# Four-layer image kernel: a head without early fillers, the first result added from its PSUM bank, and the places of all steps drawn anew

## The reference

```
x = x + moe(norm(x))        # layer 0: 2x2 patches (128 values), router over 8 experts, the best 2 of them,
                            #          (v * sigmoid(g)) @ w2[e], where v, g are the halves of patch @ w1[e]
x = x + deform(norm(x))     # layer 1: 3x3 convolution gives offsets and masks; 9 taps x 4 corners are
                            #          gathered at the offsets, weighted, multiplied by w; batch norm, relu
x = x + s4d(norm(x))        # layer 2: encoder to 256, state-space convolution (16 taps), gelu, gated linear
                            #          unit, layer norm, decoder
x = x + mixer(norm(x))      # layer 3: depthwise 7x7, channel norm, 32 -> 128 gelu -> 32, layer scale
```

## Time and profile before

| | us |
|---|---|
| runs (median, lowest, highest) | 1696.59, 1690.04, 1696.91 |
| profiled execution: its own time | 1698.67 |
| profiled execution: span from first to last instruction | 1696.9 |
| first gather starts | 58.26 |
| last gather starts | 1585.30 |
| PE, DVE, ACT, POOL busy | 1339.8, 1006.1, 541.9, 1180.7 |
| 1,152 gathers, busy and mean | 1155.8, 1.003 |

### The profile page before, as it was taken

How to read it: one execution, slowest core, us unless ns; L and a number is a source line. 1 busy time by engine, 2 the same in 40 slices (tenths; PEclk the granted TensorE clock), 3 DMA queues, 4 the chain that set the end, 5 groups by cost and what they waited for, 6 DMA issues and landing times.

```text
span 1696.9 us, 13775 instructions
## 1 busy us (share of the span) xinstructions
PE 1339.8 (79%) x4164; PEld 611.3 (36%) x4164; DVE 1006.1 (59%) x1809; ACT 541.9 (32%) x870; POOL 1180.7 (70%) x1187
## 2 busy tenths in 40 slices
PE   8778566999849958879969848789849644898797
PEld 7543233444324413324334313334224211343345
DVE  4546765544662479943655588845433794445785
ACT  2122212323332331243423412342413304244345
POOL 1477777756777777777777778777777777777700
PEclk9889877999969979989979979989869876899899
DMA  7233223421322222322332223322221112222000
GB/s 254 64 82 84 79 66 84 118 61 56 92 78 73 65 57 77 90 75 56 86 97 59 62 62 84 92 64 70 61 76 53 50 53 59 81 64 68 22 10 16
DMA packets 109609, 123.06 MB, mean 73 GB/s; under 512 B 49952, under 2 KB 85856, under 8 KB 109408
## 3 DMA queue, kind: packets, MB, share of 16 engines
q0 software_dynamic: 36864, 75.57, 15.8%
q1 hardware_dynamic: 71712, 43.40, 10.0%
q10 hardware_dynamic: 960, 3.21, 0.5%
HBM read 101.89 MB, written 9.01 MB: 65 GB/s over the span
## 4 chain that ended last, share of the span: by engine, by line
PE 37%; POOL 25%; DVE 20%; issue 10%; ACT 5%; DMA 2%; SPq 1%; DVEq 0%; POOLq 0%; ACTq 0%
POOL gt L1042 25%; PE bank L1991 7%; PE bank L2004 6%; DVE rb L1742 5%; PE bank L1941 4%; PE bank L1905 4%; PE bank L1901 3%; PE bank L1915 3%; DVE gt L1626 3%; PE bank L1974 2%; DVE he L1524 1%; PE bank L2027 1%; DVE gt L1628 1%; PE bank L2048 1%; PE bank L1805 1%
## 5 line engine op out<-in xcount | busy, mean ns | idle before, releaser
L1042 POOL DMA_INDIRECT gt<-corner_table,idx x1152 | 1155.8, 1003 | 422.3 <-issue 347.3
L1991 PE MATMUL bank<-u,wk 128*128 128x512 f32 x512 | 240.4, 614 | 3.7 <-DMA u<-sqb 3.7
L2004 PE MATMUL bank<-yg,wts 128*128 128x512 f32 x512 | 234.3, 602 | 0.4 <-DVE rb L1682 0.2
L1626 DVE TENSOR_TENSOR gt<-gt,bank 128x1152 f32<-128x1152 f32 x128 | 172.6, 1349 | 88.2 <-DMA gt<-corner_table,idx 87.1
L1905 PE MATMUL bank<-xg,w_sb 128*128 128x512 f32 (+1 forms) x256 | 135.3, 612 | 45.1 <-DVE xg L1515 23.3
L1961 PE MATMUL bank<-cst,sm 128*128 128x128 f32 x384 | 75.9, 313 | 118.1 <-DVE sm L1634 117.9
L1668 DVE SCALAR_TENSOR_TENSOR tg<-tg,ae 128x512 f32<-128x512 f32 x64 | 44.1, 692 | 198.2 <-ACT ae L1218 198.2
L1742 DVE SCALAR_TENSOR_TENSOR rb<-xp,par,rb 128x1024 f32<-128x1024 f32 x124 | 155.0, 1291 | 0.0
L1991 PEld LDWEIGHTS bank<-u,wk 128*128 128x128 f32 x512 | 97.3, 197 | 121.7 <-issue 114.7
L1524 DVE SCALAR_TENSOR_TENSOR he<-he,bank 128x512 f32<-128x512 f32 (+1 forms) x128 | 83.0, 651 | 92.0 <-PE bank L1905 88.8
L2004 PEld LDWEIGHTS bank<-yg,wts 128*128 128x128 f32 x512 | 95.2, 192 | 111.5 <-issue 109.4
(11 more groups left out here) (283 smaller groups left out, 1512.5 us busy)
## 6 DMA issues: line engine op xcount, KB each, us to landing
gt<-corner_table,idx POOLq DMA_INDIRECT x1152
tb<-gate_of_token SPq DMA_DIRECT2D x56, 256.0 KB, 4.9
u<-sqb SPq DMA_DIRECT2D x48, 128.0 KB, 2.8
corner_table<-tb SPq DMA_DIRECT2D x36, 128.0 KB, 2.7
w_sb<-w ACTq DMA_DIRECT2D x6, 512.0 KB, 7.1
xp<-x_patch SPq DMA_DIRECT2D x4, 512.0 KB, 4.4
X<-x SPq DMA_DIRECT2D x1, 1536.0 KB, 9.2
out<-X SPq DMA_DIRECT2D x6, 256.0 KB, 2.2
```

What stands on the lines that cost most here:

```text
L1042: pool.indirect_dma_start(gt[:, t % GRING, k].rearrange("p a c -> p (a c)"), None, corners, bass.IndirectOffsetOnAxis(ap=idx[s % 2][:, j, ...
L1626: ch.then(tt(rows, rows, share.unsqueeze(2).to_broadcast([P, 4 * KK, C]), ALU.mult))
L1991: op = mm(psum[b][:, :], wk[:, t, d], u4[:, g, at:at + HALF], start=t == 0, stop=t == JJ - 1 and n > 0)
L2004: op = mm(psum[B2.bank(*name)][:, :], w_glu[:, k, col + d * P:col + (d + 1) * P], yg[:, c % 2, k], start=k == 0, stop=k == NB2 - 1)
```

## The change

It has three parts; the last words of its description, on the depthwise taps, say that these stay as they were, and no line of the diff touches them.

- **Head.** `l0_norm` loses its first `keep(3, 20)`, and the one behind it goes from 10 to 5; `pass0_out` loses `keep(3, 10)`; the one ahead of the first `l1_conv` goes from 28 to 14. On VectorE the multiplications by the shares become `pass0_gated`, the first of them ahead of the last `pass0_he`. SP loads `X[:, 0]` behind the weights instead of ahead of them and `X[:, 1:]` only behind `l0_shares(1)`; the wait for it moves from `load_conv` to pass 3's `l0_tail`. Six of the 18 table clears are issued before SP waits for the gates.
- **First result.** `l0_collect(0)` goes, on ScalarE and SP: in `l0_tail` VectorE adds the four 32x256 quarters of bank 2 straight to X.
- **Places.** Most numbers of `PL` are new; pass 3's places no longer have the lower bound `h2`.

```diff
-PL = {'k1': 8.5, 'k2': 13.5, 'cut': 20, 'u1': 1.4, 't1': 2.0, 'h1': 5.5, 'u2': 5.9, 'c2': 9.5, 't2': 11.4, 'h2': 14.8, 'r3': 15.3, 'u3': 15.8, 'c3': 18.5, 'ub': 5.2, 'uc': 13.8, 'tail': 23.9, 'headend': 27.8, 'route': 26.8, 'route2': 33.1, 'bstart': 1.2, 'bend': 10.7, 'cend': 21.0, 'ahead': 16.2, 'astart': 22.4, 'aend': 31.7, 'a0head': 18.7, 'zbstart': 3.4, 'zbend': 6.4, 'zcend': 15.5, 'zahead': 16.7, 'zastart': 19.2, 'zaend': 26.5, 'zchead': 24.5, 'zcstart': 25.8, 'zcstop': 31.6, 'last2': 9, 'a0start': 19.7, 'a0end': 34, 'c30': 23.1, 'tail0': 25.1, 'headend0': 29, 'bhead': 0.5, 'head': 24.8, 'b1': 3.8, 'e3': 7, 'd3': 0.7, 'c0': 2.1, 'c1': 5.8, 'e4': 9.5, 'd4': 0.6, 'f0': 9.3, 'f1': 9.6, 'f2': 12.2, 'f3': 13, 'd5': 0.8}
+PL = {'k1': 1.57, 'k2': 9.76, 'cut': 26, 'u1': 0, 't1': 1.94, 'h1': 5.87, 'u2': 6.02, 'c2': 7.22, 't2': 9.7, 'h2': 12.8, 'r3': 10.56, 'u3': 13.02, 'c3': 19.53, 'ub': 6.18, 'uc': 13.8, 'tail': 24.74, 'headend': 28.99, 'route': 26.95, 'route2': 33.1, 'bstart': 1.11, 'bend': 10.7, 'cend': 21.96, 'ahead': 16.2, 'astart': 23.16, 'aend': 31.7, 'a0head': 20.3, 'zbstart': 0.44, 'zbend': 6.4, 'zcend': 20.18, 'zahead': 16.85, 'zastart': 21.52, 'zaend': 26.33, 'zchead': 24.85, 'zcstart': 26.43, 'zcstop': 30.35, 'last2': 9, 'a0start': 22.35, 'a0end': 32.5, 'c30': 22.05, 'tail0': 24.06, 'headend0': 28.27, 'bhead': 0.5, 'head': 26.66, 'b1': 3.8, 'e3': 7, 'd3': 0.7, 'c0': 2.1, 'c1': 5.8, 'e4': 9.5, 'd4': 0.6, 'f0': 9.3, 'f1': 9.6, 'f2': 12.2, 'f3': 13, 'd5': 0.8}
...
-    for u in range(2, PAIR):
+    for u in range(2, PAIR - 1):
         parts += value[u:u + 1] + first[u + 5:u + 6]
+    parts += [("pass0_gated", 0)] + value[PAIR - 1:] + [("pass0_gated", e) for e in range(1, NE)]
...
-        put(heads(1), (g("c2") + .2, g("c2") + .3, 1), (max(g("r3"), g("h2") + .2), max(g("u3"), g("h2") + .7), 2))
-        put(units_a(3), (max(g("u3"), g("h2") + .7), g("c30")))
+        put(heads(1), (g("c2") + .2, g("c2") + .3, 1), (g("r3"), g("r3") + .7, 2))
+        put(units_a(3), (g("u3"), g("c30")))
...
-        parts = first_pass() + [("load_conv",), ("l0_collect", 0), ("l0_tail", 0)] + head_a(0)
+        parts = first_pass() + [("load_conv",), ("l0_tail", 0)] + head_a(0)
...
-    some += [(g("c0"), *fourth[0])] + spread(taps, [(g("c1"), g("c2"), len(taps))])
+    some += [(g("c0"), *fourth[0])] + spread(taps, [(g("c1"), 9.5, len(taps))])
...
-            sp.dma_start(X[:, 0], x_v[:, 0]).then_inc(S["x0_in"], 16)
...
+                sp.dma_start(X[:, 0], x_v[:, 0]).then_inc(S["x0_in"], 16)
                 sp.dma_start(wts[:, :], weights).then_inc(S["wts_in"], 16)
                 sp.dma_start(bb[:, :, :].rearrange("p t m -> p (t m)"), places).then_inc(S["wts_in"], 16)
                 sp.dma_start(wenc[0:NB2 * C, :], w_enc[0:NB2 * C]).then_inc(S["wts_in"], 16)
-                sp.dma_start(X[:, 1:NS], x_v[:, 1:NS]).then_inc(S["x_in"], 16)
+
+            def clear_tables(t):
+
+                sp.dma_start(tables[1, t], tb[:, 0, 0]).then_inc(S["table_zero"], 16)
+                sp.dma_start(tables[0, t][:, 1:GI], tb[:, 0, 0, 1:GI]).then_inc(S["table_zero"], 16)
 
...
+                if a == 0:
+                    sp.wait_ge(S["zeros_set"], 1)
+                    for t in range(TQ // 3):
+                        clear_tables(t)
                 sp.wait_ge(S["gate_out"], 16 * (a - SPLIT + 2 if a else 1))
                 if a == 0:
                     for i in range(NE):
                         spread_share(sp, a, i)
-                    sp.wait_ge(S["zeros_set"], 1)
-                    for t in range(TQ):
-                        sp.dma_start(tables[1, t], tb[:, 0, 0]).then_inc(S["table_zero"], 16)
-                        sp.dma_start(tables[0, t][:, 1:GI], tb[:, 0, 0, 1:GI]).then_inc(S["table_zero"], 16)
+                    for t in range(TQ // 3, TQ):
+                        clear_tables(t)
...
+                if a == 1:
+                    sp.dma_start(X[:, 1:NS], x_v[:, 1:NS]).then_inc(S["x_in"], 16)
 
...
-                collect_patches(sp, a, PASSES[a][1], range(PT) if a else (0,))
+                collect_patches(sp, a, PASSES[a][1], range(PT))
 
...
-                if a == 0:
-                    collect_patches(act, a, PASSES[a][1], range(1, PT))
 
...
-            def pass0_out(e):
-                if e == 0:
-                    B0.read(dve, "both", PAIR - 1)
+            def pass0_gated(e):
+                B0.read(dve, "both", 2 * e + 1)
                 dve.wait_ge(gates_in[e], 16)
...
-                dve.wait_ge(S["x_in"], 16)
...
-                dve.wait_ge(S["o_in"], sum(len(PASSES[i][1]) for i in range(a + 1)) * PT * PT * 16)
+                if a == 0:
+                    B0.filled(dve, "out", 0, 0)
+                    for dy in range(PT):
+                        for dx in range(PT):
+                            at = (dy * PT + dx) * C
+                            xd = xv[:, :, dy, dx]
+                            op = tt(xd, psum[2][at:at + C, 0:TOK].rearrange("p (h w) -> p h w", h=H // PT), xd, ALU.add)
+                    op.then_inc(free[2], 1)
+                    B0.read(dve, "out", 0, 0)
+                    return
+                if a == SPLIT:
+                    dve.wait_ge(S["x_in"], 16)
+                dve.wait_ge(S["o_in"], sum(len(PASSES[i][1]) for i in range(1, a + 1)) * PT * PT * 16)
...
-                if s == 0:
-                    keep(3, 20)
...
-                    keep(3, 10)
+                    keep(3, 5)
 
...
-                    keep(3, 10)
                     B0.vacant(pe, "out", 0, 0)
...
-                    keep(3, 28)
+                    keep(3, 14)
```

More of the change, by code:

```diff
@@ L1785, in restart @@
                 last[:] = 0, 0
-            run(dve, dict(load_conv=load_conv, decoder=decoder, l0_norm=l0_norm, pass0_he=pass0_he, pass0_out=pass0_out,
+            run(dve, dict(load_conv=load_conv, decoder=decoder, l0_norm=l0_norm, pass0_he=pass0_he, pass0_gated=pass0_gated,
                           s4d_k=s4d_k, l0_route=l0_route,
```

## The result

The changed kernel takes 1687.03 us, the median of 20 runs (1680.94 to 1693.14), against 1697.83 of before (20 runs, 1690.04 to 1701.37): ratio 0.994, 95% interval 0.993 to 0.995. It is 0.6% faster. The prediction was 1666 (1655 to 1686), so a gain of 31 us was forecast and 11 came. The profiled execution has a span of 1684.2 us against 1696.9.

A forecast was written before the change was run, and what follows sets the result against it. Time was taken as head, gathers and tail, other engines costing only in head, tail or where a gather waits. Terms -11.2 -18.3 -1 +1 -1.5 = -31.0 took 1696.6 to 1666 us; range 1655 to 1686.

The forecast's parts named there:

- step 3 and the tail: Last step and kernel end: six taps of 0.74 us move under the gathers, image 2 closes two slots earlier; -1.5 us.
- account of lateness: Samples against gathers, tile by tile: one may end 29.4 us later than an on-time sample before GpSimd stands.
- The places of step 0: Step 0: spreading the work leaves 2 us of waits for sampled tiles instead of 20.3; -18.3 us.
- Rival (f): Step 0: pass 2's 17 units run at the 1.2 GHz level, 88 us instead of 44, giving 1710 us; chance 0.03.
- The head: Before the first gather: it starts at 47.1 us instead of 58.3; -11.2 us, bounds -8 to -12.5.
- The clock's part: Head: without fillers `pass0_h` runs its first 3 us at half speed, doing 1.5 us of work; 9.3 to 27.6.
- cost SP nothing: Head: six table clears, 3.3 us to 22.9, are issued while the gates travel and do not delay SP.
- The four adds: Head, first result into X: four 32x256 adds from the bank take 1.6 us; X ready at 36.7.
- Gathers' own duration: All steps: the gathers' own length hardly cares about taps beside them; charged 0.
- the two waits near 700 us: Steps 1 and 2: two waits of 0.8 us each can go with wider-spread taps and units; -1 us.
- the +1 for a late table: Steps 1 and 2: convolution and tables of the next step come one slot later; +1 us, bounds 0 and +6.
- The tail: After the last gather: add into X comes 1.5 us sooner, since image 2 is closed earlier; bounds 0 and -4.

The follow-up runs named there:

- e3: Changed kernel with step 2's third layer and the closings of images 0 and 1 early as before, image 2's closing and cut = 26 as changed: 1673.55 us.
- e1: Changed kernel with the nine places of step 3 as they were before the change: 1665.32 us, ratio to before 0.9821.
- e6: Kernel before the change with the nine new places of step 3, nothing else: 1715.52 us, ratio to before 1.0099.
- e8: Changed kernel with the 17 keys that place step 0 as before the change: 1707.32 us, ratio to before 1.0052.
- e4: Changed kernel with all 18 table clears behind the share fetches and an early square root on ScalarE: 1684.24 us, ratio to before 0.9927.
- e5: Changed kernel with the step-3 places of e1 and the two head edits of e4: 1660.31 us, ratio to before 0.9786.
- e10: Changed kernel with ScalarE's early square root alone, the table clears staying ahead of the share fetches: 1683.18 us, one run.
- e11: Changed kernel with keep(3, 20) instead of keep(3, 14) behind the first result: 1682.27 us, one run.
- e9: Changed kernel with VectorE's taps in steps 1 and 2, from the third on, computing 2 rows of 32, most of that sum left out: 1670.73 us, one run.
- e7: Changed kernel with the places of steps 1 and 2 as before the change: 1694.26 us, ratio to before 0.9977.

## Why the prediction was wrong

**The step that failed is the one on step 3 and the tail.** It read "Step 3: `cut` moves six taps of 0.74 under the gathers" and "Now it is closed two slots earlier ... of the 4 us only -1.5 come". I kept the account of lateness for steps 0 to 2 and stopped where the gathers no longer waited. But the last sample has no 29.4 us of room: whatever VectorE is late by there is paid in full. The budget of the ring protects gathers, not the end. Two things were not costed. Step 2's third layer was laid over slots up to 20.2 instead of 15.5 (`zcend`) and image 0's closing from 21.5 instead of 19.2 (`zastart`): TensorE busy 27 of 69 us at samples 12 to 18 and full from 22 to 28, 15 us (e3). And image 2's closing, which I counted as a gain, puts 8 us of waits ahead of the last sample (e3). Together 22.6 in the profile, 21.7 in the medians (1687.03 - 1665.32, e1), 18 in the kernel before (e6). The split into 15 and 8 rests on e3 alone; the whole is shown twice. None of my rivals had this; the range, up to 1686, ended 1 us short of the result, and the slower case that I named was another mechanism. With 22.6 in place of -1.5 the sum would have been 1666 + 24 = 1690.

**The places of step 0: right.** Waits in step 0 under 5 us (4.9), -16.3 for -18.3, and e8 gives 21.3 us of them back. Where I saw the ring at its limit, late by 30 at sample 8, it was late by 33.8, and GpSimd stood 3.2 and 1.2 us beyond issue ahead of tiles 11 and 12. The dense units did not run at the low clock: the first matmul pairs took 1.67 to 2.08 us (granted clock 0.54 from 135.5 to 146), all behind them 1.02, at 1.00 (2.4 GHz) from 146 to 184. Rival (f) did not come.

**The head: mechanism right up to X, wrong behind it, size off by 5.15 us.** The clock's part came as summed: the first two pairs of matmul records in `pass0_h` took 1.06 us each, most later ones 0.59, though the clock column says 1.00 there as it did in the earlier trace rows. 2.4 us lie before X. The gates took some 5.9 us from their issue to the first fetch instead of 4.1. The six clears, which I had let end at 22.9, held SP until 25.29; but without them it took 5.95 (e4) and 4.1 (e5), so the gates' own way may be as long. Then the fetches took 4.74 us to issue for 4.1 in the sum. So "cost SP nothing" is wrong as it stands, and that the clears cost the fetches' landing nothing looks wrong too, though e4 and e5 alone don't carry the size. I had set beside it the Trainium skill's rule (DMA: Bandwidth & Descriptors, Queues, rings and completion order) that what one sequencer issues is taken in order, worth 0.8 us of the head's gain; e4 and e5 against the profiles with clears point the same way, with a spread as large as the effect. The other 2.7 lie behind X, and I had called this stretch unchanged: 1.3 is the table load of the square root, which ScalarE had done ahead of time in before, while the patches were on their way through DMAs. The two rows of before and the two of the changed kernel:

```profile
43.15 1.28 ACT L1100 ACT_TABLE_LOAD   x1 [1.30 <-issue]
49.39 0.29 ACT L1100 ACTIVATE std<-mv,epst 32x1 f32<-32x1 f32 x1 [4.95 <-DVE mv L1463]
```

```profile
40.71 1.28 ACT L1109 ACT_TABLE_LOAD   x1 [12.20 <-DVE mv L1468]
42.00 0.29 ACT L1109 ACTIVATE std<-mv,epst 32x1 f32<-32x1 f32 x1
```

ScalarE stood idle for 12.2 us ahead of the second load, so time for it was there; the load stands behind the wait for the variance, where before it stood ahead of it. Why it changed sides no run shows; the early root of e10 puts it back. The remaining 1.2 to 1.4 is TensorE's clock: granted 0.75 on average over the first convolution of the changed kernel, 1.00 (the 2.4 GHz level) in before, e10 and e11. It goes with the gap of 1.9 us, of which the same table load is 1.3, so that the early root gave back both (e10) and longer fillers the second alone (e11); e8, with the gap and at 1.00, shows that the gap need not cost it. The Trainium skill (ScalarE: Activation LUTs, What ACT_TABLE_LOAD costs) gives 1283 ns for a load, and the trace agrees with 1.28. The page adds a drain and comes to some 2.66 us for a switch; here the path got 1.3 us shorter without it, so the measurement decides.

**The four adds: right**, 1.72 us for 1.6.

**Gathers' own duration: wrong, and to the good.** I charged nothing, by the earlier trace rows, though the row beside it (1.15 us a gather at 633 to 730) said otherwise. Measured -7.2 and -6.0 us of busy time in steps 1 and 2. e9 shows that it is the taps beside the units, and e7 that spreading them wider gives 9 us. The 14.2 us of steps 1 and 2 hid more than half of the loss at the end: that the result lies only 1 us above the range is luck, not a sum nearly right.

**Steps 1 and 2, waits and tables: the two waits near 700 us went, as forecast; the +1 for a late table did not come.** No gather waited for a table in the changed kernel; the last of step 2 was issued by 793.88, 9.4 us before the gather that needs it.

**The tail: wrong.** The add into X follows the last sample's start by 11.7 us, as before (11.6), not 1.5 sooner. The closing did leave that stretch, but the lateness brought something else into it. TensorE stood idle for 11.10 us until the last tile was sampled, and what it then ran, the turn, the 12 fillers (24 records) and `dcn`, is the chain to X:

```profile
1577.45 0.90 PE L1975 MATMUL bank<-cst,sm 128*128 128x128 f32 x3 [11.10 <-DVE sm L1651]
1578.15 4.74 PE L1822 MATMUL bank<-cst 128*128 128x128 f32 x24
1582.82 2.76 PE L1988 MATMUL bank<-st,wts 128*32 128x512 f32 x6
```

The granted clock was 0.50 in the turn (the 1.2 GHz level) and 0.58 on average in the fillers, which took 4.74 us; in before, where TensorE was busy with the closing until then, the same fillers ran at 1.00 in the 2.84 us of the sum. These 1.9 us are what ate the -1.5. e1, on time again, has 2.84 as well, and e3 and e6, late again, 4.50 and 4.75.

## What to carry to other kernels

Where a stream (here the gathers) bounds a kernel and a ring lets the other engines fall behind, keep the account of their lateness to the very end: in the middle it is free up to the ring's depth, at the last element it is paid in full. Work in the last stretch belongs as early as its inputs allow, and nothing that waits for another engine belongs ahead of the last element on an in-order engine. When a round trip is removed, list what ran under it (here a table load and the fillers that kept TensorE busy) and look in the next profile where it stands now: the load came out onto the path although its engine had been idle for 12 us.

## What the runs showed of the hardware

The length of an indirect gather's issue on GpSimd depends on what VectorE does, but not on its busy share: 0.951 us each with taps alone in 59.6 of 60 us, up to 11.3 / 9 = 1.26 us on average over a tile of the changed kernel where taps alternate with the units of layer 0, and 0.98 again when those taps touch 2 rows (281.70/288, e9). Which pair of instructions does it was not tried. And TensorE's clock after a gap of about 1.9 us in the head differed between runs of the same instructions: the first convolution took 5.11 to 5.82 us in six profiles (granted clock 0.75 in the changed kernel's) and 4.14 in a seventh (1.00, e8); after 0.55 us it took 4.14 in all four. Behind the fillers of before it took 4.14 after 2.1 us and 5.66 after 2.75 (0.72, e6). After 11.1 us of idle time at the end, 24 filler records took 4.74 us (0.58) for 2.84 (1.00).
